# Decoder kernel on one core: the written-out order of five engines' steps replaced, and 240 filler matmuls of 256 columns turned into 101 of 512

## The chip, the cores and the metric

The kernel runs on one core of a Trainium2 chip. The metric is the device time of one execution in microseconds (us), lower is better. Before the change it is 998.69 us, the median of 3 executions (998.45 to 999.51).

## The reference

Two decoder layers run over x (32 sequences of 128 tokens, width 256). After every block the sum of input and block output is layer-normed. The blocks, in order, with the letter that the kernel uses for each:

```python
x = LN(x + local_attention(x))        # Q, A: 16 heads, window of 7, extra per-window weights
x = LN(x + cross_attention(x, ctx))   # B: one head, masked
x = LN(x + expert_attention(x))       # X, Y: 8 experts, each picks 16 tokens a sequence, rotary attention
x = LN(x + decay_attention(x))        # C: one head, scores times a decay mask
x = LN(x + memory_attention(x, ctx))  # D, E, T: hot key/value chosen by argmax, 16 heads, output projection
x = LN(x + conv_ffn(x))               # F, H: int8-like rows, ternary weights, 256->1024, conv of 3, silu, 1024->256
```

## The kernel before, in words

**Tiling.** The 32 sequences are worked off in 16 groups (NG) of two. A group's activations are 128 partitions x 512 columns, so nearly every evacuation, product and copy has that form. All groups pass through the same blocks, and up to six groups (NX) are in flight.

**Engines and steps.** TensorE multiplies and transposes, ScalarE (ACT) copies out of PSUM and does Exp, Tanh and squares, VectorE (DVE) does the rest, GpSimd (POOL) a handful of tiny scale computations, SyncE (SP) the DMAs. On each engine every block is a generator, a function per letter (`windowed` is A, `cross` B, `memory` E, `feed_forward` F, `gate` H, `setup` S and so on), and each `yield` ends a step. Ordering between engines is by semaphores only.

**What sets the order.** The strings in `ORDER`, one for each engine. `walk(order, stations)` reads a string letter by letter and lets the named block go one step further. A block takes its groups one after the other. So a string fixes, for its engine, which step of which block comes next, and as the engines execute in order, a step whose semaphore is not there yet holds all that stand behind it. Here a step is called by letter, group and number in the group: F14.17 on DVE is the 18th step of the feed-forward of group 14; S4 is the fifth setup step on its engine.

**The places that matter below.**
- Start, TensorE: Q0.0 to Q0.2 are the three projections of group 0; Q1.0 and Q1.1 query and key projection of group 1 into bank_a; B0.1 the value projection of cross attention into bank_c; S4 the fifth setup step, a string of small fp32 matmuls with the biases (bank_e[3]); A0.3 the transposes of the summed windows of group 0, which need DVE's last sum and bank_a free, that is Q1.1 copied out by ACT (line 1533).
- End: E15 is the memory attention of the last group. TensorE computes logits (892, 896), ACT raises them (1769, four steps a sequence), TensorE multiplies with the values, ACT copies out (E15.9 and E15.10 on ACT), TensorE turns the blocks back (542), DVE divides (E15.8 to E15.11, lines 1389 and 1392). Then T15: transposes, copy, projection, norm. Then the feed-forward F15 of the last group and its gate H15. Beside it runs the feed-forward of group 14. It handles its hidden units in four parts: TensorE product, DVE scaling (1434), ACT middle tap (1816), DVE outer taps (1443), ACT Tanh (1821), DVE product (1453), ACT Abs (1825), DVE running maximum (1459), and at the end DVE's fold of the maximum (1491). Its gate H14 is: maximum, scale, four products (1512), the second matrix, and the norm H14.7 (1037).
- Fillers: `warm` (letter W, line 1024) issues matmuls into bank_c that nobody reads. The first may start when D15 and T13 are through, and the order string spreads them between the real steps of the tail.

Of the kernel before, what the change touches and what calls it, by code (L numbers as in the profile page):

```python
# [68 lines left out]

ORDER = {  # L70
    "PE": (
        "QQQASSASASBQSQBAQAASDABABSBBQBQXBXASAXQXAXABXBABYBYQBYYYQYBAYAXQCXCABXBXAXBAXBQYCYQCYYYBYCAYCAXBXQDAXDXD"
# [13 lines left out]
        "SQSSQQSQSSASSASASSSSSSSSSSSSAASSAASAAAAAASASAAAAAAAASASSSSSSQSSSSSQQSSSSAQSSSSAAASSSSSSABBASSSASSSAAABAA"
        "AAAAAAAAAAAAXXXXXSXXSXXAXQQQQAAAYBBAYYXAABAYAYAAAAAAAAAAAAAAAQYQQAQAXXXXXXXXAXXABBAAAAXAYYYBAAAAAYYAAAAC"
# [10 lines left out]
        "HAEAYAHAAAHHHHXXXTXXXXQXHDXDDAAFFFQXQXEEQFEEEFEEEFFBBFFFFAAFFBFFYYFFYFFAEAEFFAAAYFAYFCACAAHHAAHAAEECAAAH"
        "HHHTAAAAYHFFFXXXDDDXXXXAXXFXXEEFFEEEFEFEBEBFFFYFYYFBFFFFYYFFEFEFCCFFEEHCHHYHHHHTXXXXXHXXFFFXXDDDXFXFFFEE"
        "FFEEFEFECECEFFFFYYYFFCFFYYFEEFFFHHHHHHDDDHYEEHEETEFFFEEEEECCFFFCFFFFFFFFFFFFFDFDFEDEFEFEHHHHHHTHEEHFFFEE"  # L100
        "EEEFEFFFFFFFFFFFFFEEEEFFFFTFFHHFFHFHHHHFFFFFFFFFFFFFFFFFFHFFHHHHHHHHH"
# [1897 lines left out]
```

How the kernel before makes its waits and increments, by code:

```python
            def load_x(g):  # L412
                src = io["x"][g * T:(g + 1) * T, :].rearrange("(b t) d -> t b d", b=GB)
                if g >= NX:
                    sp.wait_ge(y_out, 16 * (g - NX + 1))
                sp.dma_start(xs[g % NX][:, :, :], src).then_inc(x_in[g % 2], 16)
# [1 line left out]
            def load_xt(g):  # L418
                if g:
                    sp.wait_ge(a_v_proj, g)
                sp.dma_start(xT0, io["xT"][g].rearrange("p (c t) -> p c t", c=DC)).then_inc(xt_in, 16)
# [1 line left out]
            def setup(_):  # L423
# [9 lines left out]
                for dst, name in ((raw_q, "raw_q"), (raw_k, "raw_k"), (q1, "wq1T"), (k1, "wk1T"), (v1, "wv1T"), (p1, "wp1"),  # L433
                                  (bqkv, "bqkv1")):
                    sp.dma_start(dst, io[name]).then_inc(factors_in, 16)
                yield
                for name in ("xmask", "wv0x"):
                    sp.dma_start(w[name][:, :], io[name]).then_inc(b_in, 16)
                yield
                for dst, name in ((gam, "gamma"), (bits, "bits")):
                    sp.dma_start(dst, io[name]).then_inc(decay_in, 16)
                yield
                sp.wait_ge(setup_pool, 6)
                sp.dma_start(wr_pad[:, :, 0:NE], io["wr"].rearrange("p (c n) -> p c n", c=DC)).then_inc(xw_in, 16)
                for name in ("cos_sin", "blk", "iota128"):
                    sp.dma_start(w[name][:, :], io[name]).then_inc(xw_in, 16)
# [42 lines left out]
            def feed_forward(g):  # L489
                sp.wait_ge(n_f.done, g + 1)
                if g == NG - 1:
```

## Time and profile before

| | |
|---|---|
| median of 3 | 998.69 us |
| the profiled execution: its own time / span | 998.45 / 996.6 us |
| TensorE busy | 925.7 us (93%) |
| VectorE busy | 855.4 us (86%) |
| ScalarE busy | 737.8 us (74%) |
| GpSimd busy | 214.8 us (22%) |
| mean granted TensorE clock | 0.990 |

Busy time is the union of an engine's instructions. A matmul's modelled end reaches into the next matmul, so busy TensorE time is an upper figure; the start-to-start distance is what a matmul costs. The 1.9 us between span and time lie before the first and after the last instruction.

### The profile page before, as it was taken

Reading aid. Unit: us, or ns where it says so; the run is one execution under the profiler, and the core shown is the slowest. Engines: PE = TensorE matmul, PEld = TensorE weight load, DVE = VectorE, ACT = ScalarE, POOL = GpSimd, SP = SyncE. Lnnn points to the kernel's source line nnn. Section 1 sums busy time; section 2 is a strip of 40 time slices with the busy share of each in tenths; the row PEclk is TensorE's granted clock in tenths of the full one; section 3 lists DMA queues with packets and bytes.
Section 4 is the critical chain, followed back from the end, with each engine's and each line's share of the span. In section 5 each row is a group of like instructions: output and inputs, shape, how many; then the busy total and the mean of one; then the engine's idle time right before and its main releaser. Section 6 shows DMA issues by size and latency. Waiting matters only on the chain.

```text
span 996.6 us, 20813 instructions
## 1 busy us (share of the span) xinstructions
PE 925.7 (93%) x7636; PEld 688.0 (69%) x7636; DVE 855.4 (86%) x2217; ACT 737.8 (74%) x1852; POOL 214.8 (22%) x469
## 2 busy tenths in 40 slices
PE   6788999999999999999999999999999999988887
PEld 4555676767777676767668676767768676766665
DVE  4887676599999999999999999989999997877877
ACT  2276556778887968877787878788787989788673
POOL 2012121303222231312222131312212131212101
PEclk9999999999999999999999999999999999998999
DMA  9932202030121203030301203030301200000000
GB/s 264 374 107 74 85 23 73 4 92 1 54 64 55 62 12 106 13 105 1 116 1 43 75 22 96 12 106 2 116 2 42 65 23 1 22 12 12 12 1 22
DMA packets 36630, 59.09 MB, mean 59 GB/s; under 512 B 6656, under 2 KB 15872, under 8 KB 36016
## 3 DMA queue, kind: packets, MB, share of 16 engines
q1 hardware_dynamic: 36528, 57.76, 18.8%
q8 instruction: 61, 1.00, 0.4%
q14 instruction: 41, 0.34, 0.1%
HBM read 28.77 MB, written 4.19 MB: 33 GB/s over the span
## 4 chain that ended last, share of the span: by engine, by line
PE 59%; ACT 16%; DVE 14%; POOL 4%; SPq 3%; issue 3%; DMA 1%; POOLq 0%; DVEq 0%; ACTq 0%
PE bank_c L506 16%; PE bank_a L506 7%; PE banks_e L506 7%; PE bank_x L506 6%; PE bank_f L506 4%; PE bank_x L717 4%; DVE neg_top L1365 3%; ACT area_e L1769 3%; ACT squares_out L1545 3%; PE banks_e L896 2%; PE bank_a L612 2%; DVE area_f L1443 2%; ACT x L1552 2%; ACT area_bx L1533 2%; SPq L474 2%
## 5 line engine op out<-in xcount | busy, mean ns | idle before, releaser
L1443 DVE SCALAR_TENSOR_TENSOR area_f<-area_f,w_convw 128x254 f32<-128x254 f32 x240 | 104.6, 477 | 6.2 <-ACT area_f L1816 4.4
L1533 ACT ACTIVATE area_bx<-bank_x 128x512 f32<-128x512 f32 (+1 forms) x140 | 68.1, 499 | 23.6 <-PE bank_x L717 7.4
L1365 DVE TENSOR_REDUCE neg_top<-banks_e 128x8 f32<-128x1024 f32 x64 | 76.2, 1219 | 8.4 <-PE banks_e L506 8.1
L1159 DVE TENSOR_TENSOR area_a<-area_a 128x512 f32<-128x512 f32 x112 | 73.3, 683 | 4.7 <-ACT area_a L1533 3.2
L1214 DVE TENSOR_TENSOR area_a<-area_a 128x512 f32<-128x512 f32 x112 | 74.5, 683 | 1.0
L1816 ACT ACTIVATE area_f<-area_f,w_convb,w_convw 128x256 f32<-128x256 f32 x120 | 65.4, 596 | 10.1 <-DVE area_f L1434 9.7
L1769 ACT ACTIVATE area_e<-banks_e 128x512 f32<-128x512 f32 x120 | 64.1, 602 | 8.4 <-PE banks_e L896 8.1
L1218 DVE TENSOR_TENSOR area_a<-area_a 128x512 f32<-128x512 f32 x96 | 65.7, 684 | 0.4
L1533 ACT ACTIVATE area_a<-bank_a 128x512 f32<-128x512 f32 (+1 forms) x80 | 44.0, 549 | 20.1 <-PE bank_a L506 15.3
L1533 ACT ACTIVATE area_bx<-bank_c 128x512 f32<-128x512 f32 x64 | 34.4, 537 | 28.6 <-PE bank_c L506 21.2
L506 PE MATMUL bank_x<-area_bx 128*128 128x128 f32 (+1 forms) x240 | 48.1, 333 | 3.9 <-ACT area_bx L1533 3.7
L1865 POOL TENSOR_TENSOR area_bx<-area_bx,minus 128x2 f32<-128x2 f32 x16 | 13.1, 818 | 179.1 <-ACT area_bx L1558 179.1
L717 PE MATMUL bank_x<-w_wqkv_e,area_bx 128*32 128x384 f32 x512 | 47.9, 492 | 0.0
L1434 DVE TENSOR_TENSOR area_f<-bank_f,area_f 128x512 f32<-128x512 f32 x64 | 43.8, 685 | 4.5 <-PE bank_f L506 4.2
L506 PEld LDWEIGHTS bank_x<-area_bx 128*128 128x128 f32 x240 | 38.2, 190 | 10.9 <-ACT area_bx L1533 6.6
L1821 ACT ACTIVATE area_f<-area_f 128x512 f32<-128x512 f32 x60 | 38.0, 634 | 7.9 <-DVE area_f L1443 7.4
L1453 DVE SCALAR_TENSOR_TENSOR area_f<-area_f 128x512 f32<-128x512 f32 x60 | 41.0, 683 | 3.3 <-ACT area_f L1821 3.1
L506 PE MATMUL bank_f<-area_f,w1q 128*128 128x256 f16 x256 | 39.1, 275 | 3.2 <-DVE area_f L1434 2.5
L1533 ACT ACTIVATE area_e<-banks_e 128x512 f32<-128x512 f32 (+1 forms) x60 | 32.1, 535 | 10.5 <-PE banks_e L537 6.4
L506 PE MATMUL banks_e<-chosen_key,chosen_q 32*128 32x256 f32 x512 | 36.7, 400 | 2.6 <-DVE neg_top L1365 1.5
L612 PE MATMUL bank_a<-area_a,w_headsum 128*32 128x256 f32 x448 | 34.1, 384 | 5.4 <-DVE area_a L1159 5.0
L506 PE MATMUL bank_c<-area_bx 128*128 128x128 f32 (+1 forms) x192 | 36.6, 328 | 1.7 <-ACT area_bx L1533 1.4
(405 smaller groups left out, 2657.5 us busy)
## 6 DMA issues: line engine op xcount, KB each, us to landing
area_a<-area_a SPq DMA_DIRECT2D x96, 224.0 KB
area_a<-in_xT SPq DMA_DIRECT2D x16, 256.0 KB, 2.9
area_bx<-in_ctxT SPq DMA_DIRECT2D x16, 256.0 KB, 3.1
x<-in_x SPq DMA_DIRECT2D x16, 256.0 KB, 3.8
area_d<-in_ctxT SPq DMA_DIRECT2D x16, 256.0 KB, 2.7
y<-x SPq DMA_DIRECT2D x16, 256.0 KB, 2.2
w_wqkv_e<-in_wqkv_e SPq DMA_DIRECT2D x1, 3072.0 KB, 10.9
area_f<-in_raw SPq DMA_DIRECT2D x2, 1024.0 KB, 12.0
```

The costliest lines, as they stand in the source:

```text
L506: last = pe.matmul(out_ap, l, r, start=i == 0 and not opened, stop=closes and i == len(pairs) - 1)
L612: last = pe.matmul(bank_a[32 * j:32 * j + 32, 0:T], w["headsum"][:, at:at + 32], product_of(wi)[:, c * T:(c + 1) * T], start=wi % 2 + c == ...
L717: last = pe.matmul(bank_x[ES * q:ES * (q + 1), 0:3 * HP], xgf[:, c, e, :], wq[:, c, e, :], start=c == 0, stop=c == DC - 1)
L1159: return dve.tensor_tensor(product_of(wi).rearrange("p (n t) -> p n t", t=P), qT0.rearrange("p c (b t) -> p (c b) t", t=P), kT0.rearrange( ...
L1214: made[wi] = own.mark(dve.tensor_tensor(v4, v4, bc(e4[:, :, wi, :], 3, DH), ALU.mult))
L1218: added = dve.tensor_tensor(vw[:, to, :], vw[:, to, :], vw[:, wi, :], ALU.add)
L1365: dve.tensor_reduce(top[:, b, r:r + 2, :, 0].rearrange("p r (par c) -> p r c par", c=DC), banks_e[:, r:r + 2, :].rearrange("p r (c par k) ...
L1434: dve.tensor_tensor(blocks(th_f[jj % 3], 2), blocks(bank_f[:, :], 2), bc(tscale_f, 1, 2), ALU.mult).then_inc(f_h, 1)
L1443: last = dve.scalar_tensor_tensor(c4[:, i, :, dst], h4[:, i, :, src], cwt3[:, 2 * jj + i, k:k + 1], c4[:, i, :, dst], ALU.mult, ALU.add)
L1533: return act.activation(dst, src, ACT.Copy)
L1769: act.activation(weights(g, b)[:, r * 4 * P:(r + 1) * 4 * P], bank_e[r][:, :], ACT.Exp, scale=float(DH) ** -0.5).then_inc(e_exp, 1)
L1816: last = act.activation(c4[:, i], h4[:, i], ACT.Identity, bias=w["convb"][:, j:j + 1], scale=cwt3[:, j, 1:2])
```

## The change

It replaces the strings for PE, DVE, ACT and POOL; the string for SP is the same. No instruction other than the fillers is added, taken away or altered, and every block still goes through its steps in its own order. What changes is how the blocks' steps are interleaved. Leaving the fillers out, 46% of TensorE's 958 steps stand at another place in the list (by 0.7 places in the mean, by 12 at most), 65% of DVE's (1.6, at most 19), 68% of ACT's (1.3, at most 18) and 40% of POOL's (at most 4). The fillers become 101 with 512 columns each, in place of 240 with 256. After the output projection T15.1 there are 44 where there were 150; before it 57 where there were 90; behind the first of the last group's four hidden-maximum transposes (F15.7 on PE), 6 where there were 39.

```diff
-WARM = 240
+WARM = 101
     "PE": (
-        "QQQASSASASBQSQBAQAASDABABSBBQBQXBX...
+        "QQQASSAASSBQQBSAQAADSBABASBBQBQXBX...
...
-        "CHECYTHDTDXHDCDFXFDFXDFCEXECFCXFECECYYEEDYEDYHDHYEYDYDEDHTECTCECDFCFEFECFCFEEDFDDEEEDHTDHTWEWWWWHWWWWWWW"
-        "EWWWWWFWWWWWFWWWWWFWWWWFEWWWWWWEWWWWWWWWWWWFWWWWWWWWWWWWWEWWWFWWWWWWEEEWWWWWWWEWWWWWTWWWWWWWWTWWWWWWWWWW"
...
+        "CEHCTYHDTDXHDDFFDFXDFXCECXEFCCXFCECEYEDYEEDYHDDYHEYDEYDDHTTECCEFCFFCFEECFCEFDEDDEEDEHDTHDTWEHWWEWFWWFWFW"
+        "WWWFWWEWWWWWEWWWWWFWWWWWWWEWWFWWEWWWWWWWWWEWEWWWWWWWWEWWWWHTWHTWWHWWWWWFWWFWWWFWWWWFFWWWWWWWFWWWWWWWWWWF"
...
                 for i in range(WARM):
-                    pe.matmul(bank_c[:, 0:D], ones_bf[:, :], bias_parts[0][:, :], start=True, stop=True)
+                    pe.matmul(bank_c[:, :], ones_bf[:, :], bc(bias_parts[0][:, :], 1, GB), start=True, stop=True)
                     yield
```

The three fragments that the prediction speaks of, read out of the strings (fillers left out):

```
start, PE   before: S3 B0.0 Q1.0 S4   Q1.1 B0.1 A0.3     after: S3 B0.0 Q1.0 Q1.1 B0.1 S4   A0.3
end, ACT    before: E15.5 E15.6 E15.7 E15.8 E15.9 F14.9 F14.10 E15.10 F14.11 T15.0 F14.12 F14.13 F14.14
            after:  F14.9 E15.5 E15.6 E15.7 F14.10 E15.8 F14.11 E15.9 F14.12 F14.13 E15.10 F14.14 T15.0
end, DVE    before: F14.16 E15.8 E15.9 E15.10 E15.11 F14.17 F14.18 F14.19 F14.20 T15.0 F14.21 F14.22 H14.0 H14.1
                    F15.0 F15.1 H14.2 F15.2 H14.3 to H14.6 F15.3 to F15.20 H14.7 F15.21 F15.22
            after:  F14.16 to F14.20 E15.8 E15.9 F14.21 E15.10 F14.22 E15.11 H14.0 to H14.4 T15.0 H14.5 H14.6
                    F15.0 F15.1 F15.2 H14.7 F15.3 to F15.22
```

On ACT, F14.9, .12 and .14 are the Abs of parts 1, 2 and 3 of the hidden units, F14.10 and .13 the Tanh of parts 2 and 3, F14.11 the middle tap of part 3; E15.5 to E15.8 are the exponentials of the second sequence. On DVE, F14.17 and .18 are the outer taps of part 3, F14.19 and .21 running maxima, F14.20 the product of part 3, F14.22 the fold.

## Rows read from the trace of the kernel before

**Rows 1.** The page: busy time, and TensorE's busy tenths in 40 slices
```profile
PE 925.7 (93%) x7636; PEld 688.0 (69%) x7636; DVE 855.4 (86%) x2217; ACT 737.8 (74%) x1852; POOL 214.8 (22%) x469
PE   6788999999999999999999999999999999988887
```

**Rows 2.** Windows: start:end, length, busy us (instructions) of each engine, clock, DMA
```profile
0.00:100.00 100.00, 77.03 (x446) 55.02 (x447) 74.12 (x193) 47.58 (x107) 17.74 (x40) 0.95 0.63 204
...
200.00:900.00 700.00, 674.77 (x5750) 503.61 (x5748) 638.73 (x1662) 562.93 (x1432) 162.40 (x344) 1.00 0.16 47
...
910.00:920.00 10.00, 7.13 (x82) 4.16 (x86) 7.56 (x19) 9.82 (x25) 2.19 (x5) 0.78 0.00 1
```

**Rows 3.** The chain that ended last, at the start: start us, us, what
```profile
29.57 1.99 PE bank_a L506 x8
31.56 3.20 PE banks_e L506 x22
34.77 3.57 PE bank_a L506 x8
...
40.95 0.50 ACT area_a L1533
...
41.59 0.64 PE bank_a L629 x4
```

**Rows 4.** Timeline of the same stretch: start, us, instructions [idle before, releaser]
```profile
31.60 0.60 ACT L1533 ACTIVATE area_a<-bank_a 128x512 f32<-128x512 f32 x1 [1.82 <-PE bank_a L506]
...
36.72 0.69 DVE L1218 TENSOR_TENSOR area_a<-area_a 128x512 f32<-128x512 f32 x1
...
40.36 0.60 ACT L1533 ACTIVATE area_bx<-bank_c 128x512 f32<-128x512 f32 x1 [8.16 <-PE bank_c L506]
```

**Rows 5.** Timeline of TensorE, idle time before single steps in the middle and at 915
```profile
422.87 1.08 PE L506 MATMUL bank_c<-area_d 128*128 128x128 f32 x8 [1.01 <-ACT area_d L1533]
...
915.19 0.76 PE L506 MATMUL bank_f<-area_f,w1q 128*128 128x256 f16 x4 [1.84 <-DVE area_f L1434]
```

**Rows 6.** Fillers, and the 512-column bias matmul: count, ns min/median/max, first and last start
```profile
L1024 PE MATMUL bank_c<-bias_parts,ones_bf x240: 272/273/283, 934.7 to 989.6; 128*128 128x256 bf16 x120
L516 PE MATMUL bank_a<-bias_parts,ones_bf x18: 376/379/390, 45.7 to 904.2; 128*128 128x512 bf16 x18
```

**Rows 7.** Timeline of TensorE in the tail
```profile
958.45 0.66 PE L537 MATMUL banks_e<-w_ident,area_e 128*128 128x128 f32 x4 [0.26 <-DVE area_e L1392]
...
972.69 2.78 PE L1024 MATMUL bank_c<-bias_parts,ones_bf 128*128 128x256 bf16 x24
```

**Rows 8.** Timeline of ACT in the tail
```profile
952.50 2.03 ACT L1769 ACTIVATE area_bx<-banks_e 128x512 f32<-128x512 f32 x4
954.47 0.60 ACT L1533 ACTIVATE area_e<-bank_x 128x512 f32<-128x512 f32 x1
...
956.34 0.60 ACT L1533 ACTIVATE area_e<-banks_e 128x512 f32<-128x512 f32 x1 [0.23 <-PE bank_x L542]
956.83 1.08 ACT L1816 ACTIVATE area_a<-area_f,w_convb,w_convw 128x256 f32<-128x256 f32 x2
...
960.16 0.62 ACT L1821 ACTIVATE area_f<-area_a 128x512 f32<-128x512 f32 x1
```

**Rows 9.** Timeline of DVE in the tail
```profile
957.97 0.42 DVE L1392 TENSOR_TENSOR area_e<-banks_e,area_e 128x256 f32<-128x256 f32 x1
958.31 1.78 DVE L1443 SCALAR_TENSOR_TENSOR area_a<-area_f,w_convw,area_a 128x254 f32<-128x254 f32 x4
960.29 0.69 DVE L1459 TENSOR_TENSOR area_a<-area_f,area_a 128x512 f32<-128x512 f32 x1 [0.20 <-ACT area_f L1825]
...
961.83 0.42 DVE L1037 SCALAR_TENSOR_TENSOR x<-banks_e,x 128x256 f32<-128x256 f32 x1 [0.24 <-PE banks_e L506]
...
983.29 0.68 DVE L1453 SCALAR_TENSOR_TENSOR area_f<-area_f 128x512 f32<-128x512 f32 x1
...
984.70 1.29 DVE L1473 TENSOR_REDUCE area_a<-banks_e 128x2 f32<-128x512 f32 x2
```

More of the change, by code:

```diff
@@ new lines @@
+        "EYDHTXDTDAHXADDQEFBFXEFBXBFXAEFBEFCXAACYEBBYECQCEYQYCHYEYECYTHDXTDHXDADADFDFQFXEBFEBXAFBEXBXFBAEBAYCEQCY"
+        "ECYECYHEDHEYCYCYTQTDAHXADXDQFDFDAEXBFEBXFBEXBXBFAEBYEFCEAYCQCYQCYECHYCYDYEXEDHATDTDHDAXDQFEFBFXEFBXBABXF"
+        "BEXEFABECYECAYCYQCYHEYQCYEHCEYTDXTADHDXDADDFEFBFXEBXFBQBXFAEBXFEBAECYACYECYECYQHECYHCEYDQTDYDTXDHDAXDABE"
+        "FQFXEFBXBFEBXAFEBFXBAACECEYQCYECQYEYHCYEYTCTYDAXDHADXDHDQDAEFBFEXFBFXBABEXEFABBXCFEQEYCYECYCHYEYCEYTCYDX"
+        "HQDXTDHADADDFQXEFBFEFBXBABXBEFBEFCXEACAYECYECYYHDECYEHCYTBTYDHXDAXDFADFDFXFEXBEBXBXEBFBEYCCFEYECEYCYXYEY"
@@ L84 @@
+        "CEHCTYHDTDXHDDFFDFXDFXCECXEFCCXFCECEYEDYEEYDYHDYHEYDEYDDHTTECCEFCFFCFEECFCEFDEDDEEDEHDTHDTWEHWWEWFWWFWFW"
+        "WWWFWWEWWWWWEWWWWWFWWWWWWWEWWFWWEWWWWWWWWWEWEWWWWWWWWEWWWWHTWHTWWHWWWWWFWWFWWWFWWWWFFWWWWWWWFWWWWWWWWWWF"
+        "WWWWWFWFWFWHWWHHWHH"
     ),
     "DVE": (
[L86 to L87 removed]
@@ L98 @@
[L98 to L101, printed above, removed]
+        "SSSQQQQSSASSSSSSAASSSSSSSAASSSSSASASASASAAAAAAAAAAASAAASSSSQSSSQSQQSSSSAASSSSSASASSSSSSSBBAASSSSASAAABAA"
@@ new lines @@
+        "AAAAAAAAAAAAXXXSXSXXXXXAXQQQQXAAAYBBYYAAAAAABYYAAAAAAAAAAAAAAYAQQQQAXXXXXXXXXXAAXBBAAAAYYYABAAAAAYYAAAAC"
+        "CAAAAAAQQQQYCAAXXXXXXXXXXAADDDXYYYEEBBAAYYEEEEEEAAAAAAABAAAAAEEAAAAAACCCEQEYQQQTAAFFFDDDAAXXXXFXXXXXFXEE"
+        "FFEEEFEEEFFFBBFFYAYAYXBAAFFFFAFAEEFFFYAYFFCCAAHHAHAAAACEEAAAAAAYHHHHTQQQQHDDDFFFAXXAXXXXXXXEEFXEFEFFEEEE"
+        "FFFFBBFFFFYYYAABFFFXFYYAAEFAAEFAACFFAACAAHHHAAAACEEAAAHHHHYATAQAHFFFDDDAQQQAXXXXXEEXXFXXEEXEEFEFFEBBFFFF"
+        "XYAAYYBFFFFAAYYFFFFAAAFFEEACACAFFAAAAAACAAAAEHHEHYAHHHQHAQTDDQQDHFAFXAXFXXXXXXXEEXEFEFEEFFEFEFFFBXBFFAAF"
@@ new lines @@
+        "FYYYFFAAFAABFAYYFFEEFCCAFAAAAAAAAHAHAHEAAECAYHHHHATHQQFFQFDDDXXAQXXXXXXXAFEEFFFXEEEEEEFFFFBFBAAFFYFXYYBA"
+        "AFFFFFFYYEEAAAAAAFFCCAAHHHAAAAEAEAAACHHAHHAYTQQHQFAFQFADDXDXXXXXXXXAAEEFXEEEEEEFFFFBBFFFXYYYFFBFFAAFFFFY"
+        "YEEAAAAAFAFCCFFAAAACAAAAAHAYAHHAEEHHQQQHHTDDDQHAFXFFXXXXXXXXEEAFXEFFFEEFBEBEEFFFAAFFXFFYBYYFFFEEFAAYYFFA"
+        "AAAFFCAHCAHHAAAAAAAAACEEAYAHHAHHTQQQQHDDDXFFFXXXXXXXAXEEXFEEEAFFFEFBBEEFFFFFAYAFFBYYFXFFFAAYEYFEFAAAAAFF"
+        "CCAAHAHHHHCAEHHAEAAAAYAAAAQTDDDQQXXQXXXHAFXXFXFXEEAXEFEEEFEEFFBBFXFFFFAAFFBFAAYYYAAFFFAAFAEEAAAYYFFCCFFA"
@@ new lines @@
+        "AAEEAAAACAHHHAAYQTHHHHAAQQQDDDXXFXXXHFXXXAFXEEAEFXEEEFEEFFBBFFFFAAFBFFYYYFFFEEFFFFYYAAAAFXAFCCAAAEEAAAAC"
+        "HYHHAAAAAHHAHHXXQXTXXXHXXDDDFFFXAAQQQEEFEXEFFFFBBEEEEFFFXFBFFAAFFYYYFFFAAFFEEAYYFAFCCAHAAHHAAAEEHHCHHAAA"
+        "ATAAYAAAAHFFFDXDDXXXXXXAXXFXFEEFFXEEFEBEBEEFFYFYYBFFFFFEYEYFFFFFCCFFEEHHHCYHHHHTXXXXXHFFFDDDXXXXFXXFFFEF"
+        "EFEEEEFEEFCCFFFFFYFYYFCFFFYEEYFFHHHHHDEDDHHYETHEEFFFEEEEFEECCFFFFFCFFFFFFFFFFFFFFEEDEDEDHHHHHHHTEEHFFFEE"
+        "EEFEEFFFFFFFFFFFFFFFFFEEFEFEHHHHHTHHFFFHFFFFFFFFFFFFFFFFFFFFHHHHHHHHH"
@@ L114 @@
-        "FCFHDFDDDXHCFFFXCFFCXECFFEEEFYEFCEFYCFDYDEYEEEDYEYDYDDDYTCHTCTHCFFFDECFCEEEFCFEFCFFFDEEFFDEEFEFEFDTDDDTT"
-        "HFFFHFEEFFEEEFFFEEEEEFFEFTFFFTTFFFFFFFFFFFHHHH"
+        "QSQQSSSAAQBSBQASQASDSABASBBASSBSSQSBSBSXQSSXABASQXASSXBSXSABBAYYBYQYBSYBSQYBAYAYXQCXACBXABXBAXSYQBCYQYYY"
+        "BCBYACYCXCXBAQDADXDXADDDXBYYBAYBQCYEEEEEBEQCBYCEEYEECCYEACTCDTDYATDQXYFFDXFDDDFAABFBFXBXEFFFBXEBEEEABEFC"
+        "FFQYCFBFCFEEYEECYEYCYCQYTDCDXYATDTHDFXDDDHFAFYBFQAXBFFBXEFFFBEEEXBECFFFBEAYCFFBAYCFQEEEEYCEYCYCYQDCTDYTD"
@@ new lines @@
+        "TAHYXDXAFDDDFQFHBAFBBXFFXEBFXBFFEEEEYFCAEFFABCYFQFCBFYEEYECECEYCYDCQDYTDXTYATHDXDDDHAFFQFBAFBXFFXBFEFFEF"
+        "CEEEXABFFCABEYBFFYCFQBYCEEEYEYECYCTYDCXQDTHTDAYHXFDFADDDFQAFBBFXFFBXFEFBXAFBEEEEFFBECYFFAQCBYCFEEYEECYED"
+        "YCYCTQCYDATHTXDHXYFFDQDDDFABFABXBFEXFBFXFBFEEEEFAYECFFCABQYFFYCBFCYCEYECYEQECEDYDTXADTDTHXADDDFFHFYBAQFB"
+        "BFXFFBXEFFBXFEEEEFFAECBYCFFYAFCYQBYCYEEEEYCECQTCYDDTXADTHXYDHDDDFFAFBFABBXFFQBXFFFEXBFEEEEAFFCEYBCAFFYFC"
+        "YEEEEYCCEQYCYDCQTDBYDXTDAXYDDDTHBAFFHFAQFBBXFEFBXFFFEBEEEXFACBAEFFFCYQBFCEEEYEFYCEYYCTYQCCDAXYDTDXATDQDD"
@@ L116 @@
+        "DAHFFFBHFBYXBAFFEBXFEEBFFFEEXBCAFEFFBYFCEEFYCQYEEYCEYCYCDTCXDQYXDTATHDFDDDFAFHBAFYBQBFXFFBXEBFFEEEECFFXA"
+        "FEBCFFAYBFCYEEYECEYDECYCTYCBTDYXTDHXAFYFDFDDDFAAXBFFBXHFBEXBFFEECFBEECYEBFFYCEYEFFYEEXFYCECYTCDCYDTXTDYF"
+        "FFDFDDDXCFFHCXHFCFFCXCEFFFEEEEYCFFECDFYYDYEEEEYDEYDYDDDTYTCTCHFFFCHFECEFCFFEEECFFFCEFDFDEEFFEEFDEDTDDDTT"
+        "FFFHFHEFFEEFEEFFFEEEFEFEFFEFTTTFFFFFHFFFFFFHHH"
     ),
     "POOL": (
-        "ABBABBYYABBYCCAYBBYCCTYABBYCCTHHYABBYHCCTAYHBBYCCYHTHABBYHCCTYHABBHYCCTYHABBYCCTHAYHBBYCCHTYHABBHYCCYTAH"
@@ L119 @@
-        "BBYCCHTAHYBBYCCHTYHABBYCCHTHYABBYCCHYTHCCYYHHTCCHTHTHHHH"
+        "ABBABBYYABBYCCYABBYCCTAYBBYCHCTYHABBHYCCTYHABBYCCYTHHABBYCCHTYHABBYCCHYTHABBYCCHTHYABBCYHCYTHABYHCCBTYHA"
+        "BBYCCTHYAHBBYCCHTHAYBBYHCCTYHABBYCCYTHHCCHYYTHCCHTHTHHHH"
     ),
```

33 lines of the change are left out of this document (3 added, 30 removed).

## The prediction

> **What bounds the kernel now.** I read the page first. TensorE is busy 93% of the span, DVE 86%, and the slices show where it is not the same everywhere: TensorE is below 9 tenths at both ends only [rows 1]. The windows put numbers on that. From 200 to 900 us TensorE is busy 674.77 of 700 us, so all its idle time there is 25.2 us, or 3.6%; in the first 100 us it is idle 23.0 us, and there the granted clock is 0.95 [rows 2]. A new order can't take away work. It can only take away idle time, and in the middle there is little. So three stretches have to be read apart: the start, where one chain of single steps sets the pace; the middle, where TensorE's queue is nearly dense; and the tail behind 930 us, where the last group has no other group to hide it and each wait of its chain is paid in full. For the start I followed the chain of waits, for the middle the idle times in TensorE's timeline, for the tail the timelines of three engines side by side.
>
> **The start: S4 goes behind Q1.1 and B0.1.** In the chain, TensorE does Q1.0 at 29.57, then S4 for 3.20 us, then Q1.1 in 3.57 us, then B0.1; ACT copies B0.1 (0.60, from 40.36) and then Q1.1 (0.50), and only now is bank_a free for A0.3 at 41.59 [rows 3, 4]. ACT stood idle 8.16 us before that copy, and DVE had its last window sum done at 36.72 + 0.69 = 37.41, so neither of them is the cause [rows 4]. With S4 out of the way, Q1.1 can start when ACT has copied Q1.0, at 31.60 + 0.60 = 32.20 [rows 4]. It takes 1.99 us like Q1.0 if the clock is full and 3.57 us as it did here [rows 3]. I take the first, for S4 (one-column matmuls, mostly) was the work ahead of the fall: Q1.1 until 34.2, B0.1 (about 1.99) until 36.2, the two copies until 37.3, S4 from 36.2 to 39.4. A0.3 is then held by S4 and starts near 39.4, 2.2 us sooner. If Q1.1 still runs at half clock, S4 ends at 41.0 and the gain is 0.6 us. If the low clock falls on A0.3 and the projection behind it instead, 0.6 us of the gain go, since 8 such matmuls cost 1.6 us more at the low level [rows 3]. From A0.3 on the chain is made of the same single steps. S4 and its followers (the decay table, the biases) are needed by a setup step on ACT that comes some 13 us later, so its delay by 4.8 us is covered. I found one more exchange in ACT's string, the squares of B0 ahead of two setup steps, each some 0.7 us; ACT is dense there, so I count it at nothing. The start gives -2.2 us, between -0.6 and -3.
>
> **The middle.** About 40 idle times of over 0.35 us make up most of TensorE's loss. The largest is 1.01 us, D5.5 waiting for ACT's copy of the step right before it [rows 5]. In the new string F4 stands between those two, which would fill 0.6 us of it. In about a dozen of the 40 the new string puts another block's step into the gap, some 7 us in all. But the trace can't show the gaps that the same string opens: where two steps of one block now follow each other, the same 0.5 to 1 us is paid anew. I can't price the two against each other, so I bound them: closing the dozen and opening none gives -7, opening as many as half the present idle time costs +12, with the likely value near 0, since the two strings have the same kind of neighbourhood and the displacement is 0.7 places in the mean. I take 0 ± 3.
>
> **The tail, attention of the last group against the feed-forward of group 14.** Today ACT raises the second sequence's four blocks in one go from 952.50, copies out at 954.47 and again at 956.34, and does the middle tap of part 3 after that, at 956.83 [rows 8]. DVE's last division is at 957.97, its outer taps of part 3 follow at 958.31 [rows 9]. After: on ACT, Abs 1 stands before the exponentials (0.5 us), Tanh 2 before the last of them, and the middle tap before the first copy. The exponentials end near 955.7, the middle tap runs 955.6 to 956.7 (now 956.83 to 957.9). DVE does the outer taps 956.7 to 958.5 (1.78, rows 9). Tanh 3, 0.62 us [rows 8], ends at 959.1, and the second copy (E15.10) stands behind it: 959.7 instead of 956.9. TensorE's blocks turn back in 0.66 [rows 7], to 960.4. Meanwhile the product of part 3 (0.68, as the one at 983.29) allows Abs 3 at 959.9 to 960.5, the running maximum (0.69) ends at 961.2 [rows 9], and a short reciprocal, the fold and the division E15.11 (0.42 by its row) end at about 962.0. Today E15.11 ends at 957.97 + 0.42 = 958.39 [rows 9]. So T15's transposes start 3.6 us later than their 958.45 [rows 7]. The stretch from there to the norm at 961.83 [rows 9] is as long as before: of H14's steps that now lie in it, three tiny ones come before the projection and two products (1.4 us) beside it. The bounds: 0, if group 14's feed-forward comes to this place that much sooner; and +5, if the delayed Abs and copies also catch the turned blocks of the first sequence.
>
> **The tail, what comes back.** H14.7, two additions of some 0.45 us, stands today between 983.29 + 0.68 and the last maxima at 984.70 [rows 9]. After, it lies in the shadow of F15's start, where DVE waits. The last maxima then start at 984.0, when DVE is free, if their transposes are there; fillers and the second matrix of group 14 stood before these transposes, and both are gone from that place but for one filler each. I take -0.7 us. Tail: +3.6 - 0.7 = +2.9.
>
> **The fillers.** One of today's costs 0.109 us: 24 of them span 2.78 us, of which the last has 0.27 [rows 6, 7], so (2.78 - 0.27) / 23. All 240 fill 26.2 us. The 512-column form lasts 379 ns against 273 [rows 6]: 256 more columns cost 0.106, so one costs about 0.215 us, and 101 fill 21.7 us. They stand in waits; what they cost is the part of one that a real step finds before it, up to 0.1 us now and up to 0.2 us after, on some 15 steps that lie on the chain, less what fewer of them give back. I take 0, between -0.5 and +1.5. What the page of the Trainium skill says against thinning them is weighed with the rivals.
>
> **Sum.** -2.2 + 0 + 2.9 + 0 = +0.7 us on the profiled execution's own 998.45: 999.1. The median is 0.24 above that execution; I split the difference of the two bases by naming 999.0 us. A measurement of this kernel can tell about 0.2% (2 us) from no change, so the forecast is: no change that shows, with a range of its own of 997 to 1001.
>
> **Rivals.**
> 1. *The middle or the stretch around 915 gets denser, faster.* Today TensorE waits 1.84 us at 915.19 for DVE's scaling [rows 5], and the clock falls with it: the window from 910 has 7.13 of 10 us busy and 0.78 granted [rows 2]. The new string starts group 13's feed-forward two steps sooner. If that closes the wait and keeps the clock, it gives the 1.8 us and about 1 us of matmuls at the full level. With half of the dozen gaps of the middle closed for good (-3) the time is 999.1 - 5.8 = 993.3. Against it: D15.0, which today lies ahead of this wait, is moved behind it, so nothing new fills it.
> 2. *The tail's delay doesn't appear, faster.* If group 14's feed-forward reaches 950 us some 3 us sooner because it is ahead of the attention everywhere on DVE, only the start's gain and the -0.7 stay: 998.45 - 2.9 = 995.6.
> 3. *The tail's delay appears and the start's gain is lost, slower.* The place is E15.10 behind Tanh 3 on ACT, the price 3.6 us as worked out; it decides if the start yields less than 1.5 us (low clock on Q1.1, or a DMA or setup step that is late anyway). Time: 998.45 + 2.9 = 1001.4, more if the middle gives nothing back.
> 4. *The clock falls in the last 10 us, slower.* Behind F15.7 only 6 fillers (1.3 us) stand where 39 (4.2 us) did. By the rows, the clock fell around 915 behind a wait that nothing filled [rows 2, 5], and at the start behind one-column matmuls [rows 3]. If it falls here, eight fp32 matmuls cost 1.6 us more [rows 3], and the work that is left there is about as long again, partly beside DVE's products: +1.5 to +2, so 1001 on top of the forecast. The Trainium skill, "TensorE: Matmul & The Clock Gate", Part 1, states that the throttled clock is the default and that activity releases it, so that idle stretches of TensorE bring half rate back. That speaks against this change, and the row at 910 agrees with it (0.78); by that rule the thinner fillers alone would make the time some 2 us longer, while by the density of the rest of the tail nothing would change.
>
> **How the numbers follow.** Forecast (start and tail cancel, within 2 us) 0.34. Rival 1: 0.22. Rival 2: 0.14. Rival 3: 0.19. Rival 4: 0.11. That gives faster 0.36, same 0.34, slower 0.30. The middle's bounds are wide (-7, +12); its likely ± 3 added to rival 2 gives 993, and added to rival 3 1004.5. These are the ends of the range, and I leave 0.1 out on each side.
>
> **What would show it.** Right at the start: A0.3 (L629) near 39.4 instead of 41.59, and ACT's wait of 8.16 us cut. In the tail: from the first filler to the last division (L1392) 3 to 4 us more than today's 958.39 - 934.7 = 23.7 us [rows 6, 9], the second copy of line 1533 directly behind a Tanh; from the connect norm (L1037, bn_sums_e) to the end 0.7 us less. In the middle: TensorE's idle from 200 to 900 within 3 us of 25.2. The prediction is wrong if that idle moves by more than 3 us, if the distance in the tail doesn't grow, or if the clock is low behind 970 us.

## The result, and the profile after

The changed kernel takes 1013.73 us (median of 4 runs, 1013.01 to 1014.0) against 999.0 (4 runs): a ratio of 1.0145, 95% interval 1.0129 to 1.0162. It is 14.7 us slower, where "no change that shows" was forecast, and far outside the range. The profiled execution took 1010.35 us (span 1008.4). In the changed kernel's file every line number is one lower than before.

The page, to be read against [rows 1]: work and busy shares are nearly the same, and the PE row differs most at its end (887885 where 988887 stood).

```profile
PE 924.4 (92%) x7497; PEld 674.0 (67%) x7497; DVE 856.6 (85%) x2217; ACT 735.8 (73%) x1852; POOL 215.5 (21%) x469
PE   6778999999999999999999999999999999887885
```

The windows (start:end, length, busy us of PE, PEld, DVE, ACT, POOL, clock, DMA), of the changed kernel:

```profile
0.00:100.00 100.00, 74.94 (x448) 54.52 (x449) 74.24 (x194) 48.33 (x109) 19.51 (x40) 0.97 0.63 204
200.00:900.00 700.00, 671.16 (x5689) 497.98 (x5689) 634.06 (x1647) 557.94 (x1421) 160.06 (x339) 1.00 0.15 46
780.00:943.00 163.00, 143.93 (x1233) 104.73 (x1233) 131.91 (x347) 130.13 (x328) 32.39 (x76) 0.99 0.05 16
910.00:920.00 10.00, 8.36 (x77) 6.50 (x81) 8.28 (x18) 8.06 (x21) 2.12 (x6) 1.00 0.08 28
```

and of the kernel before, the window that no row of the prediction covers:

```profile
780.00:943.00 163.00, 149.16 (x1297) 110.03 (x1295) 135.48 (x360) 133.71 (x338) 32.44 (x84) 0.98 0.05 14
```

From 200 to 900 TensorE idles 28.8 us where it idled 25.2. In the 163 us from 780 on, the stretch in which the last groups run out, it is busy 5.2 us less (3.8 of these are fillers, which the kernel before already issues from 934.7 on), and DVE and ACT are each busy 3.6 us less. The low clock at 910 is gone there, but only to come back at 925, behind a wait of the same length:

```profile
925.35 0.40 PE L891 MATMUL banks_e<-area_e,w_quarters 32*128 32x128 bf16 x16 [1.83 <-ACT area_e L1768]
```
```profile
920.00:930.00 10.00, 7.54 (x77) 5.15 (x74) 8.46 (x20) 9.53 (x25) 2.30 (x5) 0.83 0.00 1
```

How far each TensorE step of the changed kernel starts behind the same step before (median over the steps of ten us, worked out from both traces), and the same for kernels told of below:

```
us in the kernel before     40     80    150    300    390    460    600    760    850    900    940    970
changed                   -2.4   -0.2   -0.7   -0.8   -1.2   +1.3   +0.4   +1.1   +5.4   +9.2   +8.2  +11.9
start only (until 150)    -0.8   +1.1   +1.8   +1.8   +1.8   +2.1   +2.1   +2.1   +2.1   +2.1   +2.8   +2.8
until 750                 -2.6   -0.2   +0.5   +0.3    0.0   +2.5   +1.5   +2.2   +2.2   +2.2   +2.2   +2.2
drain only (770-938)         -      -    0.0    0.0      -      -   +0.2   +0.3   +5.5   +9.2   +9.1   +9.1
half drain (770-849)         -      -      -      -      -      -      -   -0.6   +4.6   +4.6   +4.5   +4.5
one step moved (775)         -      -      -      -      -      -      -   -0.5   +0.5   +0.5   -1.3   -1.3
three stretches           -0.5   -0.3   +0.7   -0.6   -1.1   -1.1   -1.7   -1.7   -1.7   -1.7   -1.7   -1.7
```

So the 12 us of the profiled pair arise in the main in two places: +7 from 770 to 940, +3.7 in the tail. The middle has its share too. From 150 to 750 us the changed kernel and the three others with its order there (parts 3 and 7) all lose 1.6 to 1.8 us: 2.5 between 390 and 460, in part made up elsewhere. The start can't be read from one trace: at 150 us five executions with the new start stand between -0.7 and +1.8, nine with the old one between -0.6 and +0.8.

### The profile page after: what moved, and what is told of

Same layout as the page of the kernel before. It is cut to its first block, busy times and chain, and to the rows that moved or that the text cites. A ratio compares the mean times of both kernels' runs of the same rounds, so it can differ in the third digit from the quotient of the medians.

```text
span 1008.4 us, 20535 instructions
## 1 busy us (share of the span) xinstructions
PE 924.4 (92%) x7497; PEld 674.0 (67%) x7497; DVE 856.6 (85%) x2217; ACT 735.8 (73%) x1852; POOL 215.5 (21%) x469
## 4 chain that ended last, share of the span: by engine, by line
PE 60%; ACT 17%; DVE 14%; issue 3%; POOL 3%; SPq 2%; DMA 1%; DVEq 0%; POOLq 0%; ACTq 0%
PE bank_c L505 16%; PE banks_e L505 8%; PE bank_a L505 8%; PE bank_x L505 6%; PE bank_f L505 3%; PE bank_x L716 3%; ACT area_e L1768 2%; PE banks_e L895 2%; ACT area_bx L1532 2%; ACT squares_out L1544 2%; PE bank_a L611 2%; ACT x L1551 2%; DVE area_f L1442 2%; DVE neg_top L1364 2%; PE bank_c L536 2%
## 5 line engine op out<-in xcount | busy, mean ns | idle before, releaser
L505 PE MATMUL bank_a<-area_a,w_wq 128*128 128x256 f32 x128 | 34.0, 413 | 5.8 <-DMA w_wq<-in_wq 4.1
## 6 DMA issues: line engine op xcount, KB each, us to landing
area_f<-in_raw SPq DMA_DIRECT2D x2, 1024.0 KB, 10.9
```

Source lines behind the costliest of these rows:

```text
L505: last = pe.matmul(out_ap, l, r, start=i == 0 and not opened, stop=closes and i == len(pairs) - 1)
```

## The experiments

Each kernel ran on one chip with the kernel before beside it. "Until T" means: old and new string were cut on each engine at the place nearest T where both have worked off the same set of steps, and joined there. Times vary from execution to execution with the granted clock: of 17 of the kernel before, one took 997.44 us at a mean clock of 0.994 and one 1002.41 at 0.986, and a fit over all 17 gives 0.48 us for each 0.001 (over the 84 executions that stand beside all the kernels below, 0.52). Where a few tenths matter I give the mean "at clock 0.990" by that slope beside the ratio; for the kernel before it is 999.0 to 999.4, chip by chip, for the changed one 1011.9. Such a mean takes out what a kernel itself does to the clock as well, so it is of no use for the fillers.

**1. The start alone.**
```diff
-order: old
+order: new until 150 us, then old
```


> The new strings until about 150 us on TensorE, VectorE, ScalarE and GpSimd, the old ones and the 240 fillers from there on. Theory (where the time is lost: nowhere before 750 us): A0.3 comes about 2.6 us sooner than 41.59, but SyncE waits for S4 before it starts the ctx and x loads, and by 80 us little of it is left: -0.5 us, 998.5, between 997 and 1000. Rival (my prediction's first term): the 2.2 us stay until the end, 996.8.

1000.01 us, ratio 1.0005 (0.9990 to 1.0019). The 2.2 us don't arrive: they lie outside the interval. One reason stands in the changed kernel's chain of waits (start, us, what; SPq is SyncE's issue of DMAs):

```profile
34.29 1.73 PE bank_c L505 x8
36.02 3.22 PE banks_e L505 x22
39.62 0.43 SPq L485
40.09 0.43 SPq L415
...
43.44 1.86 SPq L479
45.35 0.54 SPq L473
...
53.97 5.45 DMA area_a<-in_xT
59.46 3.40 PE bank_a L505 x8
```

S4, the 22 matmuls at 36.02, is what SyncE waits for before it loads raw2 (line 458 of the kernel before). Behind that wait stand the ctx load (485), five x loads (415), another ctx load (479), twelve shift transfers (473) and the xT load for the next queries. The next query projection starts at 59.46.

**2. S4 alone, and S4 with SyncE's string.**
```diff
 PE
-S3 B0.0 Q1.0 S4 Q1.1 B0.1 A0.3
+S3 B0.0 Q1.0 Q1.1 B0.1 S4 A0.3
 SP (second kernel only)
-QSSSSBSASSSSQQSSSSSDAAAAABQQBQQ...
+QSSSSBSASSSSQQSSSSSDAQQAAAABBQQ...
```


> The kernel before with one step moved: S4 on TensorE behind Q1.1 and B0.1. Theory (SyncE is held by S4 before it may start the ctx and x loads, and these stand ahead of the shift transfers): A0.3 comes at about 39.2 instead of 41.59, the shifts of group 1 start near 45.4 although the values are out at 43.2, and the end moves by -0.5 to -1: 998.2. Rival (my prediction's first term): the end moves by -2.2, 996.8.

998.96 us, ratio 1.0006 (0.9989 to 1.0023); at clock 0.990 it is 998.7 against 999.0. A0.3 comes at 39.64 and the shifts at 45.90, as the theory says. But how much of A0.3's lead is the edit's? Here are Q1.0 and A0.3 in this kernel, and then in the kernel of part 4, whose start is the old one:

```profile
30.00 1.89 PE L506 MATMUL bank_a<-area_a,w_wq 128*128 128x256 f32 x8
...
39.64 0.66 PE L629 MATMUL bank_a<-w_ident,area_a 128*128 128x128 f32 x4
```
```profile
29.31 1.89 PE L506 MATMUL bank_a<-area_a,w_wq 128*128 128x256 f32 x8
...
34.33 1.99 PE L506 MATMUL bank_a<-area_a,w_wk 128*128 128x256 f32 x8
...
39.54 0.63 PE L629 MATMUL bank_a<-w_ident,area_a 128*128 128x128 f32 x4 [1.27 <-ACT area_a L1533]
```

From one to the other it is 9.64 us with S4 moved and 10.23 with S4 at its old place, where Q1.1 (34.33) ran at full clock too. In [rows 3, 5] it was 12.02. So the edit is worth 0.6 us by this pair of traces, and 1.8 us of the lead came from one execution's low clock: of ten profiles with the old start two show Q1.1 at half clock, eight don't.

> As the kernel with S4 moved, and in SyncE's string the shift transfers of group 1 and the xT load behind them stand ahead of four of the five x loads and the ctx load of cross attention. Theory: the shifts start near 43.2, the xT load near 52, Q2.0 near 57.5 instead of 61.33, and about 2.4 us stay until the end: 996.6 (995.5 to 997.5). Rival: the ctx load of cross attention, now late, or the x loads beside the shifts cost what is won: 998 to 999.

1000.96 us, ratio 1.0013 (0.9999 to 1.0027); at clock 0.990 it is 999.9 against 999.0. The rival holds. The shifts went out at 42.76 and the xT load at 51.70, some 3 us sooner, and it was no use. Its chain of waits on TensorE:

```profile
47.62 0.31 PE bank_f L506 x2
47.93 2.35 issue
50.28 2.26 PE bank_c L506 x8
```

D0.0, at 50.28, needs the ctx load for memory attention. SyncE issued it at 39.17, behind S4, and it took 11.0 us to land, so it was there at 50.2, where D0.0's wait ended. In the kernel with S4 alone moved the same load took 8.3 us, in the kernel before 10.9, but from 37.72 on, so that it was there at 48.6 and D0.0, at 50.65, didn't wait for it. A lead of 2.9 us is cut to 0.4. This execution also had half clock from 48.4 to 55.2, and its steps stand 2.1 us late at 150 us, so the trace can't price the rest.

**3. Everything before 750 us.**
```diff
-order: old
+order: new until 750 us, then old
```


> The new strings until about 750 us, the old ones and the 240 fillers behind. Theory (start and middle together cost next to nothing, the +1.1 us that the changed kernel is late at 750 us is carried to the end): 1000.1 (999 to 1001). Rival (the state in which the old drain is entered matters, and the new order before it costs more than the trace shows): 1002 or more.

1001.24 us, ratio 1.0015 (1.0001 to 1.0029): +1.5 us, or +1.3 at clock 0.990 (1000.7 against 999.4). That is a little over the theory's range of 999 to 1001 and short of the rival's 1002. Start and middle cost little, and behind 750 us the displacement stays at +2.2 until the end: the old drain doesn't mind the state in which it is entered.

**4. The drain.** First the whole of it, then its first half.
```diff
-order: old
+order: old until 770 us, new until 938 us (second kernel: 849 us), then old
```
(Where the strings join again the first kernel has four fillers fewer, 236.)


> The new strings only from about 770 to 938 us (the last groups draining), the old ones before and after. Theory: the order of this stretch alone costs the 6.5 us by which the changed kernel falls back there (+1.7 us at 750, +8.2 at 943): 1005.5, between 1003 and 1008, with VectorE's idle of some 5 us near 905 that follows the connect step T13 placed ahead of E14.0. Rival: the delay comes from the different state in which the drain is entered (the new order before 750), and this order alone costs under 2 us: 999 to 1001.

1006.66 us, ratio 1.0072 (1.0058 to 1.0086). The order of this stretch costs 7 us by itself, whatever stood before; at clock 0.990 it is 1007.7, 8.5 us over 999.2. The idle time of DVE that was expected near 905 is there, with T13 first and the reduction of E14 at 909.58 behind it (before: 899.27); the longest wait that DVE had there before was 2.01 us:

```profile
908.08 0.42 DVE L1037 SCALAR_TENSOR_TENSOR x<-bank_c,x 128x256 f32<-128x256 f32 x1 [5.01 <-PE bank_c L506]
```

> The new strings only from 770 to 849 us, the old ones before and after. Theory: the 5.2 us lost by then are carried to the end, 1004.3 (1003 to 1005.5), unless the clock spell at 915 us falls away (then 1.9 less in that execution). Rival: the loss is due to the unfinished new order, and the old one behind it wins some back: 1001 to 1002.

1004.47 us, ratio 1.0063 (1.0046 to 1.0079): nothing is won back. The same F13.4 that stands in [rows 5] at 915.19 and the same norm that stands in [rows 9] at 961.83 come 4.57 and 4.54 us later here, with the same idle times ahead of them:

```profile
919.76 1.04 PE L506 MATMUL bank_f<-area_f,w1q 128*128 128x256 f16 x4 [1.84 <-DVE area_f L1434]
```
```profile
966.37 0.42 DVE L1037 SCALAR_TENSOR_TENSOR x<-banks_e,x 128x256 f32<-128x256 f32 x1 [0.24 <-PE banks_e L506]
```

What such a loss looks like, at 770 to 776 us in the first of the two kernels, on ACT and then on TensorE:

```profile
774.79 0.63 ACT L1825 ACTIVATE area_f<-area_f 128x512 f32<-128x512 f32 x1 [0.54 <-DVE area_f L1453]
775.32 0.39 ACT L1557 ACTIVATE area_bx<-area_bx 128x128 f32<-128x128 f32 x1
```
```profile
776.24 0.44 PE L542 MATMUL bank_c<-w_ident,area_bx 128*128 128x128 f32 x2 [0.99 <-ACT area_bx L1558]
```

The exponential of B14 (1557) was done at 773.45 before. Now an Abs of F10 stands ahead of it, waits 0.54 us for DVE's product, and TensorE in turn waits 0.99 us for the exponential. Others of this kind in the same trace:

```profile
885.16 0.66 PE L730 MATMUL bank_x<-w_ident,area_bx 128*128 128x128 f32 x4 [1.09 <-DVE area_bx L1306]
...
925.38 0.40 PE L892 MATMUL banks_e<-area_e,w_quarters 32*128 32x128 bf16 x16 [1.83 <-ACT area_e L1769]
930.74 0.63 PE L537 MATMUL bank_c<-w_ident,x 128*128 128x128 f32 x4 [1.51 <-ACT area_d L1533]
```

Is it that few groups are left in flight? For the first part of the loss, no. In the trace of the kernel before, group 15 begins at 725 us and group 10 does its last feed-forward product at 805, so until then six groups are in flight, as many as in the middle, and TensorE is nearly always busy. Yet the half-drain kernel has lost 2.8 of its 5.2 us by then (-0.6 at 764, +2.2 at 804).

```profile
770.00:805.00 35.00, 34.19 (x312) 24.73 (x311) 34.38 (x87) 29.96 (x76) 7.97 (x16) 1.00 0.19 60
```

**5. One such exchange by itself.**
```diff
 ACT
-B14.2 X13.2 F10.4 F10.5 B14.3 X13.3 F10.6 E11.0
+B14.2 X13.2 F10.4 F10.5 F10.6 B14.3 X13.3 E11.0
```


> The kernel before with one step of ScalarE moved by two places at 775 us: F10.6 (a Tanh that waits for VectorE) ahead of the exponential B14.3 and the copy X13.3, as in the changed kernel. Theory (in a written-out order nothing behind a late step catches up): B14.4 on TensorE comes about 1.5 us later than 774.45, and the whole rest up to the end by 1 to 1.5 us: 1000.2, with the displacement constant from 800 us on. Rival (idle time behind it absorbs it, single exchanges are harmless and only the many together cost): under 0.3 us at the end.

(By its line, 1825, F10.6 is an Abs, not a Tanh.) 1000.05 us, ratio 1.0008 (0.9994 to 1.0021). In the trace the step behind it comes late by 1.0 us, a third less than expected, and all steps from 780 to 914 us stay late by exactly that (-0.51 before, +0.52 behind, in the table). Then 1.9 us come back at once, and the windows of before and of this kernel say from where:

```profile
910.00:930.00 20.00, 15.30 (x128) 9.03 (x128) 15.84 (x40) 17.46 (x39) 2.19 (x5) 0.83 0.00 1
```
```profile
910.00:930.00 20.00, 13.43 (x135) 8.20 (x132) 17.45 (x44) 18.28 (x42) 2.19 (x5) 1.00 0.00 1
```

The same steps behind the same wait ran at the full level in this execution. Over 12 runs the mean at clock 0.990 is 999.6 against 999.0, so the exchange costs about 0.5 us; the ratio alone can't tell it from nothing, nor from the 1.0 of the trace.

**6. The tail alone, and what is in it.**
```diff
-order: old
+order: old until 943 us, then new (fillers: twice as many of 256 columns as the new string has of 512)
```


> The new strings only from about 943 us on, with the new positions of the fillers but 256-column fillers, two for each of the 512-column ones, so that the filled time is the same; the old strings before. Theory (my prediction's third term): the second copy of E15 behind the third Tanh costs 3.6 us, the gate's norm H14.7 gives 0.7 back: 1002, between 1001 and 1003.5. Rival 1: the delay was there only since group 14 came late already, and the tail alone costs 0 to 1: 999 to 1000. Rival 2: the thin fillers behind the last maxima also let the clock fall in the last 10 us, another 1.5 to 2 us: 1004.

1004.94 us, ratio 1.0062 (1.0048 to 1.0076): more than the theory, as in rival 2. The displacement goes from +0.3 at 943 to +4.0 at 970: +3.7. Two variants of this kernel take it apart.

```diff
 PE, fillers ahead of
-H14.2 4   F15.0 10  F15.1 4  F15.4 0  F15.7 10  F15.8 2   F15.9 2  H15.0 2   H15.1 4
+H14.2 17  F15.0 13  F15.1 5  F15.4 7  F15.7 19  F15.8 19  F15.9 4  H15.0 10  H15.1 7
```


> As the kernel with the new order from 943 us on, with 63 more 256-column fillers in the idle times of TensorE behind 965 us (13 ahead of H14.2, 3, 1, 7 and 9 ahead of F15.0, .1, .4 and .7, 17 and 2 ahead of F15.8 and .9, 8 and 3 ahead of H15.0 and .1). Theory (the thin fillers let the clock fall, and that is what this tail costs beyond 3.7 us): the half-clock spell near 988 us is gone, 1002.5 (1001.5 to 1003.5). Rival: the clock falls for another reason, 1004.9, or the fillers stand in the way, 1005.5.

1002.95 us, ratio 1.0046 (1.0029 to 1.0062): 2.0 us less by medians, 1.6 by ratios, by filling idle time alone. The two intervals overlap, so the times by themselves don't prove it; the traces do: from 980 us to the end the displacement grows by 2.0 us in the first kernel (+3.2 to +5.3) and by 0.2 in this one (+4.2 to +4.4). The windows of the tail without and with them:

```profile
985.00:1003.00 18.00, 7.38 (x36) 4.71 (x36) 8.49 (x20) 3.31 (x8) 1.55 (x5) 0.68 0.09 29
```
```profile
985.00:1003.00 18.00, 8.95 (x72) 6.64 (x72) 9.48 (x22) 3.31 (x8) 1.54 (x5) 0.89 0.09 30
```

and TensorE's last maxima and last products in both, without and with:

```profile
986.80 0.66 PE L978 MATMUL banks_e<-w_ident,area_f 128*128 128x128 f32 x4 [2.02 <-DVE area_f L1453]
...
988.00 1.03 PE L978 MATMUL banks_e<-w_ident,area_f 128*128 128x128 f32 x4 [0.33 <-DVE area_f L1453]
...
992.04 0.58 PE L1008 MATMUL bank_a<-w2q,area_f 128*128 128x256 f16 x2
```
```profile
987.79 0.66 PE L978 MATMUL banks_e<-w_ident,area_f 128*128 128x128 f32 x4 [0.17 <-DVE area_f L1453]
...
988.99 0.66 PE L978 MATMUL banks_e<-w_ident,area_f 128*128 128x128 f32 x4
...
992.40 0.38 PE L1008 MATMUL bank_a<-w2q,area_f 128*128 128x256 f16 x2
```

Behind an idle time of 2.02 us four matmuls take 1.03 instead of 0.66, two products 0.58 instead of 0.38. With the clock kept, the displacement in this trace is +1.26 at 943, +4.97 at 970 and +4.40 behind H14.7: +3.7 and -0.6. That agrees with what the Trainium skill says in "TensorE: Matmul & The Clock Gate", Part 1, that idle stretches bring half rate back.

```diff
 PE, fillers ahead of
-E15.5 4  E15.6 18  E15.7 2  E15.8 16
+E15.5 0  E15.6 6   E15.7 0  E15.8 8
```


> As the kernel with the new order from 943 us on, without 26 of the 40 fillers ahead of E15.5 to E15.8 (4, 18, 2 and 16 become 0, 6, 0 and 8). Theory (the second copy behind the third Tanh is what delays T15): T15.0 comes only some 0.8 us sooner than 962.43, by what the fillers ran over E15.8: 1004 (1003 to 1005). Rival (the fillers ahead of the last attention products are the cause): T15.0 3 us sooner, 1002.

1004.04 us, ratio 1.0054 (1.0033 to 1.0075). In the changed kernel fillers ran 1.3 us over E15.6 and 0.7 over E15.8, so they looked guilty. Without them the tail still loses 3.7 us (+1.4 at 943, +5.1 at 970), and TensorE waits at both places. They are cleared: T15's time is set by ACT and DVE. The rows of ACT in the changed kernel, with the second copy directly behind the third Tanh, and of DVE with the last division:

```profile
966.75 0.63 ACT L1820 ACTIVATE area_f<-area_a 128x512 f32<-128x512 f32 x1 [0.85 <-DVE area_a L1442]
967.29 0.58 ACT L1532 ACTIVATE area_e<-banks_e 128x512 f32<-128x512 f32 x1
```
```profile
969.87 0.42 DVE L1391 TENSOR_TENSOR area_e<-banks_e,area_e 128x256 f32<-128x256 f32 x1
```

Before, they stood at 956.34 and 957.97 [rows 8, 9], the whole being 8.2 us earlier there: 967.29 - 956.34 - 8.2 = 2.8 for the copy, 969.87 - 957.97 - 8.2 = 3.7 for the division.

**7. The fillers exchanged between the kernels.** The changed order with the old fillers, the old order with the new ones (as many ahead of each TensorE step as there), and the changed kernel with its idle times filled.
```diff
-WARM = 101   (512 columns; changed kernel)
+WARM = 240   (256 columns, ahead of the steps as in the kernel before)
```


> The changed kernel's strings with the old fillers: 240 of 256 columns, as many ahead of each TensorE step as in the kernel before. Theory: the thin fillers cost clock, above all in the runs without a profile (3 us more than the profiled one at a lower mean clock); with dense ones the time is 1013.7 - 3 = 1010.7, between 1009 and 1012, and the half-clock spells at 994 and 1004 us are gone. Rival: the fillers' density costs nothing and gives nothing, 1013.7 (1013 to 1014.5).

1013.04 us, ratio 1.0141 (1.0123 to 1.0158): no gain. The mean clock rose from 0.988 to 0.993, worth 2.5 us by the slope above, and at 970 us the steps stand 15.1 us late against 11.9 in the changed kernel: the fillers stand ahead of steps that in this order don't wait.

```diff
-WARM = 240   (256 columns; kernel before)
+WARM = 101   (512 columns, ahead of the steps as in the changed kernel)
```


> The kernel before with the fillers of the changed kernel (101 of 512 columns, as many ahead of each TensorE step as there). Theory: thin fillers let the clock fall near the end (mean clock 0.003 lower) and in return stand less in the way of real steps; together 0 +-1: 999.0 (998 to 1000). Rival 1: the clock alone counts, 1000.5 to 1001. Rival 2: the delay by fillers alone counts, 997.5.

1006.42 us, ratio 1.0067 (1.0049 to 1.0085): all three theories missed. The displacement is +0.2 at 930 and +5.9 at 970, and in part for the same reason: nine fillers, from 955.35 to 957.39, stand ahead of E15.6, which in the kernel before waited only 0.18 us behind E15.5. Both kernels say the same: a filler list belongs to its order. What thinness alone does, neither shows.

```diff
 PE of the changed kernel, fillers ahead of
-H14.2 2  F15.0 5  F15.4 0  F15.7 5  F15.8 1   H15.0 1  H15.1 2
+H14.2 9  F15.0 6  F15.4 3  F15.7 9  F15.8 10  H15.0 5  H15.1 3
```


> The changed kernel with 29 more 512-column fillers in the idle times of TensorE behind 973 us (7 ahead of H14.2, 1 of F15.0, 3 of F15.4, 4 of F15.7, 9 of F15.8, 4 of H15.0, 1 of H15.1). Theory (the clock term found in the tail alone holds in the changed kernel): the half-clock spell near 994 us is gone, 2 us less, 1011.7 (1011 to 1012.7). Rival (the changed kernel's end is set by delays only, or the fillers run over real steps): 1013.7 or more.

1011.73 us, ratio 1.0119 (1.0096 to 1.0142), mean clock 0.991 instead of 0.988. By medians that is the 2.0 us expected, but the interval overlaps that of the changed kernel (1.0129 to 1.0162), and from 980 us to the end its trace wins back only 0.5 us on the changed kernel's (+0.2 against +0.7). It fits the clock term, it doesn't prove it.

**8. Only the stretches in which the changed kernel gained.**
```diff
-order: old
+order: new in 195-295, 310-385, 470-602 (first kernel: also 668-702) us, else old
```


> The kernel before with the new strings only in four stretches in which the changed kernel gained on it: 195 to 295, 310 to 385, 470 to 602 and 668 to 702 us. Theory (each stretch's gain or loss belongs to its own order and is carried unchanged to the end): -1.3, -1.1, -0.4 and -0.5, together -3.3: 996 (995 to 997.5), with a constant displacement between the stretches. Rival (gain and loss are exchanged between neighbouring stretches, so that cutting them apart loses it, or the clock gives it back): 998.5 to 1000.

997.52 us, ratio 0.9980 (0.9967 to 0.9993). In the trace the four stretches give -1.3, -0.5, -0.6 and +0.4, constant in between. The fourth had been a gain only against the late steps ahead of it.

> The kernel before with the new strings in three stretches, 195 to 295, 310 to 385 and 470 to 602 us (the fourth one, which lost 0.4 us where it had gained in the changed kernel, is left out). Theory: 0.4 us less than with four, about 2.4 us less than the kernel before at the same clock: 996.7 (995.5 to 998). Rival: the clock spells around 915 us take it back, 998.5 or more.

995.47 us, ratio 0.9960 (0.9946 to 0.9975), a small gain, but clear of 1 by its interval; at clock 0.990 it is 996.3 against 999.4, and 2.3 us of that are the stretches' (the last row of the table: +0.7 to -1.7). D5.5 and the norm of [rows 5, 9], 422.87 and 961.83 there, stand at

```profile
421.81 0.97 PE L506 MATMUL bank_c<-area_d 128*128 128x128 f32 x7 [1.01 <-ACT area_d L1533]
```
```profile
960.14 0.42 DVE L1037 SCALAR_TENSOR_TENSOR x<-banks_e,x 128x256 f32<-128x256 f32 x1 [0.24 <-PE banks_e L506]
```

## Why the prediction was wrong

The parts, timed against the kernel before, add up to the whole within their error:

| part | forecast | measured alone |
|---|---|---|
| start and middle, until 750 us | -2.2 | +1.5 |
| drain, 770 to 938 us | (within 0 ± 3) | +7.2 |
| tail: order | +2.9 | +4.6 (timed, with its idle times filled; +3.1 in its trace) |
| tail: clock behind thin fillers | 0 (rival 4: +1.5 to 2) | +1.6 (by ratios; +2.0 by medians; 1.8 in the traces) |
| sum | +0.7 | 1.5 + 7.2 + 4.6 + 1.6 = 14.9; the whole kernel: 14.7 |

Each part is known to about 1.4 us and the sum to about 2.4, so an agreement to 0.2 us is luck. It doesn't hang on the clock, though: at clock 0.990 start and middle, drain and tail give 1.3 + 8.5 + 2.8 = 12.6 (the clock's share of the tail taken out), the whole kernel 12.7.

- **The step that failed is the middle's**: "I take 0 ± 3 ... since the two strings have the same kind of neighbourhood". For 150 to 750 us it was within its bounds (+1.6 to 1.8 in four traces). But the term stood for all that lies between start and tail, and nothing else in the sum speaks of 770 to 938 us, except rival 1 for the place at 915. There the new order costs 7.2 us by time, 8.9 in the trace. What the runs show in place of "the same kind of neighbourhood, so near 0": a step that is put behind a late one on ACT or DVE is paid in TensorE time (1.0 us for one exchange), and such costs need not be balanced by gains. The text's own upper bound for the middle, +12, would have held it, so the mechanism was named and its size taken at nothing by a likeness that nobody had measured. The sign that the text gave did come: TensorE's idle from 200 to 900 is 3.6 us more, over its limit of 3, and 2.8 of these lie behind 800.
- **The start, -2.2.** A0.3 came at 39.15, as forecast (39.4), and yet the term was wrong twice: the start alone measured +0.5 us (-1.0 to +1.9). "I take the first, for S4 ... was the work ahead of the fall" took the clock of one execution for an effect of S4; at equal clock the move is worth 0.6 us, the lower end that the text gave for another reason. And "its delay ... is covered" named a step on ACT and forgot SyncE, which waits for S4 with 20 issues behind that wait. Even with the shifts taken ahead of those, a ctx load that was issued behind S4 and landed at 50.2 us stopped the gain.
- **The tail's order, +3.6 and -0.7**: right in size (+3.7 and -0.6 in the traces; from the first filler to the last division it is 27.4 us instead of 23.7), and the named cause, the second copy behind the third Tanh, stands in the trace. That it and not the fillers sets T15 is shown; that nothing else of the exchange has a share is not.
- **The fillers, 0**: wrong by some 2 us, as rival 4 had it, in its place and size. (F15.7, which the count of fillers there goes by, is the second of the four maximum transposes; behind the first, F15.6, stand 11 where 51 stood.)
- **Rival 1** was half right: the clock at 910 is 1.00 and F13.4's wait fell from 1.84 to 0.63 us, but in a stretch that by then was 9 us late, and both came back at 925. **Rival 3** had both its conditions met and was still 12 us short, since it too had no drain. Rival 2 fell.
- The sum names 999.0, but its two bases give 999.15 and 999.4; halfway is 999.3. It changes nothing here.

Not settled: which exchanges in the drain cost how much, and why this stretch has no gains to set against them. One exchange was measured (0.5 to 1.0 us). In the trace of the half-drain kernel the loss comes in several steps (+2.3 us by 786, +2.8 by 804, +3.5 by 820, +5.2 by 849), so no single exchange explains it. Fewer groups in flight may add to it behind 805; before that there are not fewer.

## What to carry to other kernels

In this program, whose order is written out for each engine, nothing absorbed a delay behind the start: from 150 us on it is carried on to a hundredth of a microsecond, and so is a gain, until the clock or a changed order alters it. (Before 150 us it is not so: of leads of 0.5 to 2.5 us at 40 us, in eight executions with the old start, 0.8 to 2.0 us are gone at 150.) So price a new order stretch by stretch and leave no stretch to a likeness with the others. Test it by cutting old and new order together where both have done the same steps: this finds the bad stretch and lets the good ones be kept. Fillers have to be placed anew for each order, as many as fit the idle time that its trace shows.
